# Weighted expert rows added to their tokens' rows by indirect DMAs, in place of stored rows and gathers

## What is computed

```python
x = x + cross_attention(layernorm(x), ctx)            # 16 heads, q and k with rms norm
h = layernorm(x)
# mixture of experts: E = 64 experts, K = 8 for each token, inner width 192
scores = softmax(h @ gate_weight.T)
topk_w, topk_idx = top_k(scores, 8);  topk_w = topk_w / sum(topk_w)
x = x + sum over k of topk_w[k] * (silu(h @ w_gate[e_k]) * (h @ w_up[e_k])) @ w_down[e_k]
# second layer
x = x + attention of layernorm(x) to the 256 context rows of its batch, masked
x = x + ternary feed-forward of layernorm(x), inner width 1408
```

## Time and profile before

| | |
|---|---|
| median of the runs | 1608.38 us (1607.07 to 1610.81, 3 runs) |
| the profiled execution | 1613.86 us |
| its span, first to last instruction | 1612.1 us |
| mean granted PE clock in the span | 0.936 of full |
| PE busy | 1428.4 us, 89% of the span |
| DVE, ACT, POOL busy | 1032.6, 905.1, 615.0 us (64%, 56%, 38%) |
| DMA queue of SP's loads and stores | 197.31 MB, 34.6% of 16 engines' span |
| DMA queue of POOL's indirect DMAs | 77.61 MB, 15.9% |

### The profile page before, as it was taken

The page is one execution under the profiler, slowest core; times in us unless marked ns, Lnnn a source line. Parts: engine busy times, 40 slices in busy tenths (PEclk is TensorE's granted clock), DMA queues, the critical chain, the costliest instruction groups (busy, mean ns, idle before and its releaser), DMA issues. The chain is left out here.

```text
span 1612.1 us, 37709 instructions
## 1 busy us (share of the span) xinstructions
PE 1428.4 (89%) x8673; PEld 1200.5 (74%) x8674; DVE 1032.6 (64%) x2067; ACT 905.1 (56%) x2048; POOL 615.0 (38%) x704
## 2 busy tenths in 40 slices
PE   7998899999843999999999999999943599999999
PEld 5887566667622898888888898888841488888888
DVE  5555488876696576777676765666635466676633
ACT  4554598873384566666666666666621244444442
POOL 1222287761142322322232232232226566666321
PEclk9999699999855999999999999999975799999999
DMA  6221592001171587778777877877537444444200
GB/s 209 85 85 53 213 359 90 2 5 53 53 307 57 180 261 270 269 252 283 261 278 255 284 236 252 269 255 240 194 129 249 131 144 141 124 125 130 78 13 28
DMA packets 93281, 278.16 MB, mean 173 GB/s; under 512 B 12757, under 2 KB 12886, under 8 KB 92502
## 3 DMA queue, kind: packets, MB, share of 16 engines
q1 hardware_dynamic: 68950, 197.31, 34.6%
q0 software_dynamic: 23680, 77.61, 15.9%
q10 hardware_dynamic: 576, 2.36, 0.4%
HBM read 209.07 MB, written 76.81 MB: 177 GB/s over the span
## 5 line engine op out<-in xcount | busy, mean ns | idle before, releaser
L1183 POOL DMA_INDIRECT xg<-h_rows,idx x168 | 183.9, 1095 | 467.5 <-PE m_x L1211 458.2
L1226 PE MATMUL m_g<-wgu_high,bxTh 128*128 x660 | 236.5, 358 | 3.7 <-DVE bxTl L1299 3.7
L1226 PE MATMUL m_g<-wgu_low,bxTh 128*128 x660 | 223.9, 339 | 0.0
L1226 PE MATMUL m_g<-wgu_high,bxTl 128*128 x660 | 223.8, 339 | 0.0
L1629 PE MATMUL f_g<-x4T_high,ffn_gu 128*128 128x256 f32 x704 | 177.0, 293 | 14.2 <-issue 12.2
L1299 DVE TENSOR_TENSOR bxTl<-m_x,bxTh 128x512 fp32r<-128x512 f32 x166 | 114.7, 691 | 88.4 <-ACT bxTh L1368 63.9
L1629 PE MATMUL f_g<-x4T_low,ffn_gu 128*128 128x256 f32 x704 | 169.9, 282 | 0.0
L1386 ACT ACTIVATE y<-m_y 128x512 f32<-128x512 f32 x164 | 98.1, 598 | 113.5 <-PE m_y L1246 87.3
L1061 DVE TENSOR_TENSOR wgu_low<-raw_gu,wgu_high x61 | 107.3, 1758 | 82.6 <-ACT wgu_high L1051 69.7
L1520 POOL DMA_INDIRECT G<-y_rows,slot x128 | 132.8, 1038 | 56.5 <-issue 50.5
L1246 PE MATMUL m_y<-wd_high,hidTm 128*128 x328 | 144.9, 442 | 7.6 <-issue 5.6
(11 more groups left out here) (264 smaller groups left out, 3310.6 us busy)
## 6 DMA issues: line engine op xcount, KB each, us to landing
raw_gu<-in_exp_gu SPq DMA_DIRECT2D x64, 768.0 KB, 6.6
y_rows<-y SPq DMA_DIRECT2D x164, 256.0 KB
raw_d<-in_exp_d SPq DMA_DIRECT2D x64, 512.0 KB, 7.4
y_rows<-zero SPq DMA_DIRECT2D x64, 256.0 KB, 3.4
ffn_gu<-ffn_gu_words SPq DMA_DIRECT2D x1, 5632.0 KB
raw_c<-in_ctxT SPq DMA_DIRECT2D x16, 256.0 KB, 2.7
X<-in_x SPq DMA_DIRECT2D x4, 1024.0 KB, 5.5
h_rows<-h SPq DMA_DIRECT2D x16, 256.0 KB, 2.0
```

The source lines that it names most:

```text
L1183: eng.indirect_dma_start(xg[:, u, :].bitcast(F32), None, h_dram, bass.IndirectOffsetOnAxis(ap=idx[half][:, u:u + 1], axis=0)).then_inc(s_g ...
L1226: m = eng.matmul(pg[u % 2][:, 0:2 * I], xT[l][:, u % 2, c, :], W.gu[r][:, buf * DC + c, :], start=c == 0 and n == 0, stop=c == DC - 1 and ...
```

## The change

In place of rows of experts stored once and gathered eight times a token, each expert's row is multiplied by its token's weight as ACT moves it out of PSUM, and added in DRAM to the row of its token.

- There are two sums in DRAM, `sums[0]` and `sums[1]`, of 2048 rows and 128 more. `attend` zeroes sum 1 and the extra rows; `route` stores X into sum 0 (16 more stores of 256 KB).
- `h_dram` has rows of 576 values: behind the 512 of h stand the token's 64 weights, one for each expert. `place` divides the exponentials L by their total (a product on POOL, where the marks were) and stores them there. DVE's search for the weights is gone; the total and its reciprocal come ahead of the lists. Padding rows now name one of the 128 extra rows, each its own (two more short operations for `blk_tok`).
- `experts`: a gather brings 576 values. POOL copies the column of the block's expert to `weight`; ACT scales by it. `y` has four slots and a fifth, in the space of X. In step b POOL issues the scatter-add of block b - 4, the weight copy of b and the gather of b + 4, in this order. Blocks with even u go to sum 0, with odd u to sum 1; a scatter waits until the last one to the same sum has landed. SP's stores are gone. POOL has four index tiles in place of two, and its loop holds four groups.
- `finish`: SP loads both sums of each tile by plain DMAs (32 of 256 KB): batch 0's first, 1's behind the small loads, those of 2 to 7 behind `load(1)`. DVE adds the two, one operation of 128x512 for each tile (16 in place of 128), and `find_exact` stands behind batch 0's norm. POOL has no DMAs there.

The core of the diff:

```diff
@@ attend, sync
-            for n in range(NBLK - T * K // P):
-                eng.dma_start(rest[n], zero[:, :]).then_inc(s_rest, 16)
+            for n in range(NT + 1):
+                eng.dma_start(sums[1][bass.ts(n, P), :], zero[:, :]).then_inc(s_rest, 16)
...
@@ route, sync
+                dveX.wait(eng, t, "x")
+                eng.dma_start(sums[0][bass.ts(t, P), :], X[:, t, :]).then_inc(s_sum, 16)
                 actH.wait(eng, t, "h")
-                eng.dma_start(h_dram[bass.ts(t, P), :], h[:, t % HBUF, :]).then_inc(s_h[t % HBUF], 16)
+                eng.dma_start(h_dram[bass.ts(t, P), 0:D], h[:, t % HBUF, :]).then_inc(s_h[t % HBUF], 16)
@@ place, gpsimd
-            eng.tensor_tensor(marked[:, :, :], mask16[:, :, :], order[:, :].unsqueeze(1).to_broadcast([P, NT, E]), ALU.mult).then_inc(s_mark, 1)
+            eng.tensor_tensor(L[:, :, :], L[:, :, :], winv[:, :].unsqueeze(2).to_broadcast([P, NT, E]), ALU.mult).then_inc(s_weight, 1)
@@ place, sync
+            eng.wait_ge(s_weight, 1)
+            eng.dma_start(h_dram.rearrange("(n p) d -> p n d", p=P)[:, 0:NT, D:D + E], L[:, :, :]).then_inc(s_weight, 16)
@@ place, vector
-            link(eng.tensor_copy(slot8[:, :, :], slot_f[:, :, :]))
+            eng.wait_ge(s_exp, 1)
+            link(eng.reduce_sum(total[:, :], e8[:, :, :], axis=AX.X))
+            link(eng.reciprocal(winv[:, :], total[:, :]))
...
-            words = L[:, :, :].bitcast(I32)
-            for n in range(2):
...
-                for t in range(NT):
-                    last = eng.max(found[n][:, t, :], both[:, t, :])
...
-            link(eng.tensor_tensor(blk_tok[:, :], plist[:, 1:NTAB + 1], below, ALU.subtract))
+            link(eng.tensor_tensor(listed[:, :], plist[:, 1:NTAB + 1], below, ALU.subtract))
+            link(eng.tensor_scalar(empty[:, :], listed[:, :], 0.0, part_f[:, 0:1], ALU.is_equal, ALU.mult))
+            link(eng.scalar_tensor_tensor(blk_tok[:, :], listed[:, :], float(T), empty[:, :], ALU.add, ALU.add))
@@ experts, sync
-                eng.dma_start(y_dram[bass.ts(b, P), :], y[:, u % 2, :]).then_inc(s_y[u % 2], 16)
@@ experts, gpsimd
+                poolW.wait(eng, (i - 1) * GB + u, "weight")
...
+            def weighted(i, u):
+
+                b = i * GB + u
+                e = eng.value_load(blk_tab[0:1, bass.ds((b + 2) * 2, 1)], min_val=0, max_val=E - 1)
+                eng.wait_ge(s_g[u], (i + 1) * 16)
+                actY.wait(eng, b - GB, "y")
+                apart(eng, s_apart)
+                poolW.done(eng.tensor_copy(weight[:, u:u + 1], xg[:, u, bass.ds(e + D, 1)].bitcast(F32)), "weight")
+
+            def scatter(i, u, at, last=False):
+
+                actY.wait(eng, i * GB + u, "y")
+                if not (isinstance(i, int) and i == 0 and u < 2):
+                    eng.wait_ge(s_y[u % 2], i * 32 + u // 2 * 16)
+                apart(eng, s_apart)
+                eng.indirect_dma_start(sums[u % 2], bass.IndirectOffsetOnAxis(ap=idx[at][:, u:u + 1], axis=0), y[:, GB if last and u == GB - 1 else u, :], None,
+                                       compute_op=ALU.add).then_inc(s_y[u % 2], 16)
+
+            def group(i, at, first):
+                for u in range(GB):
+                    if not first:
+                        scatter(i - 1, u, (at - 1) % IDX)
+                    weighted(i, u)
+                    gather(i + 1, u, (at + 1) % IDX)
+                name(i + 2, (at + 2) % IDX)
...
+            def later(i, at, last):
+                if not last:
                     with eng.If(i < groups):
+                        group(i, at, False)
+
+                with eng.If(groups > i - 1):
+                    with eng.If(groups < i + 1):
                         for u in range(GB):
+                            scatter(i - 1, u, (at - 1) % IDX, True)
@@ experts, scalar
                 peY.wait(eng, b, "y")
-                if stored is not None:
-                    eng.wait_ge(s_y[u % 2], stored)
-                actY.done(eng.activation(y[:, u % 2, :], py[u % 2][:, :], ACT.Copy), "y")
+                poolW.wait(eng, b, "weight")
+                if added is not None:
+                    eng.wait_ge(s_y[u % 2], added)
+                actY.done(eng.activation(y[:, u if at is None else at, :], py[u % 2][:, :], ACT.Copy, scale=weight[:, u:u + 1]), "y")
@@ finish, sync
+            def tokens(b):
+
+                for i in TI:
+                    t = b * TPB + i
+                    if b > 0:
+                        eng.wait_ge(s_g[i], 32 * b)
+                    eng.dma_start(X[:, t, :], sums[0][bass.ts(t, P), :]).then_inc(s_g[i], 16)
+                    eng.dma_start(G[:, t, :], sums[1][bass.ts(t, P), :]).then_inc(s_g[i], 16)
+
+            tokens(0)
             eng.dma_start(open8[:, :, :], a["mask"].unsqueeze(0).to_broadcast([P, B, S])).then_inc(s_m, 16)
...
+            tokens(1)
             eng.dma_start(Wdn[:, :, :].rearrange("p f d -> p (f d)").bitcast(F32), ffn_d).then_inc(s_ffn, 16)
             peC.wait(eng, 0, f"r{TPB - 1}")
             load(1)
+            for b in range(2, B):
+                tokens(b)
@@ finish, gpsimd
-            gather(0, places)
             Chain(nc, ctx, "f_poolc", eng)(eng.memset(minus_half[:, :], -0.5))
-            gather(1, places[:4])
             deviations_a(0)
-            gather(1, places[4:])
             deviations_4(0)
             deviations_a(1)
-            gather(2, places)
@@ finish, vector
-                dveA.done(eng.scalar_tensor_tensor(X[:, t, :], G[:, i, k, :], w8[:, t, k:k + 1], X[:, t, :], ALU.mult, ALU.add), f"k{k}_{i}")
+                    dveA.done(eng.tensor_tensor(X[:, t, :], X[:, t, :], G[:, t, :], ALU.add), f"sum{i}")
...
-            find_exact()
-            add(0, adds)
+            add(0)
             moments_a(0)
             scales_a(0)
             negatives(0)
-            add(1, adds[:6])
+            find_exact()
+            add(1)
             maxima(0)
```

More of the change, by code:

```diff
@@ L1166, in _ @@
                             one(i * GB + u, u)
-            for u in range(2):
-                eng.wait_ge(s_y[u], groups * 32 + 16)
-            apart(eng, s_apart)
         @block.gpsimd
@@ L1804, in one @@
                         beside[f](b + 1)
-                    if more2:
-                        add(b + 2, adds[n:n + ADDS.get(f, 0)])
-                        n += ADDS.get(f, 0)
+                    if more2 and f == 2:
+                        add(b + 2)
                 if more2:
```

170 lines of the change are left out of this document (67 added, 103 removed).

## The result

The changed kernel takes 1658.26 us (median of 4 runs, 1658.01 to 1662.04), against 1607.72 for the kernel before on the same chip: a ratio of 1.0318, 95% interval 1.0296 to 1.0341. It is slower; 1580.6 was forecast. The profiled execution has a span of 1656.0 us (before 1612.1), its mean granted PE clock is 0.934. The medians are 50.5 us apart and the spans 43.9, because the profiled execution of the kernel before was 6.1 us above that median. Cut at the same instructions in both traces, the difference of 43.9 us splits into

The account below looks back on a forecast made before the run. TensorE (PE) was taken to bound the experts' stage at 4.035 us a block, but not the stages around it. Terms -6.5 + 6 + 3.5 - 14.9 - 13.9 - 2.0 = -27.8 took 1608.38 to 1580.6 us, range 1562 to 1660.

Parts of the forecast that it names:

- 1, place: Between routing and experts: DVE's extraction of weights by bits goes, so the experts start earlier, -6.5 us.
- 2, experts: Experts' stage: POOL, DMA engines and scatter chain all stay below 4.035 us a block; +6 us charged for bursts.
- The chain's term: Experts' stage: a block costs at least half a scatter's issue-to-landing time L, taken as 5.5 us, half 2.75.
- The DMA term: Experts' stage: DMA engines' work per block for weights, gather and scatter, 3.22 to 4.12 us, taken as 3.6.
- rival B: Experts' stage: DMA engines fill, a second pass for adding makes a block 4.29 us, +41, 1616 us; chance 0.10.
- C, POOL is full: Experts' stage: an adding scatter costing over 2.6 us fills POOL, 4.75 us a block, +115, 1690 us; chance 0.07.
- A: Experts' stage: the scatter chain binds from L = 8.5 us; at 9.1 a block takes 4.55, 1658 us; chance 0.16.
- 3, the stage's end: End of the experts' stage: the last scatter lands later than a store did, +3.5 us (0.4 to 9).
- 4, start of the last stage: Last stage before its first feed-forward product: adds no longer wait for gathers, -14.9 us (-12 to -18).
- 5, batch 0: Last stage, batch 0: without gathers on POOL the 10.13 us idleness goes, -13.9 us (-8 to -15).
- 6, other batches: Last stage, later batches: PE already covers the adds, so removing gathers and adds gains little, -2.0 us (0 to -6).
- D: Batch 0: something other than POOL's queue holds the product back, so 13.9 us stay, 1594 us; chance 0.07.

Follow-up runs that it names:

- e1: Changed kernel with the weight copy and its register load moved from POOL to DVE, two blocks earlier in its order: 1625.0 us.
- e16: Changed kernel with POOL's order altered: weight copy before the scatter, then the gather: 1630.9 us, ratio 1.0171 to the kernel before.
- e3: Changed kernel with four sums in place of two, half of the experts' rows left out of the output: 1637.1 us.
- e6: Changed kernel with the weight copy on DVE and four sums, half of the experts' rows left out: 1595.6 us.
- e5: Changed kernel with DVE and ACT splitting only one of four gate and up chunks and one of two down chunks, output wrong: 1626.9 us.
- e10: Changed kernel with short splits on DVE and ACT and four sums, output neither the experts' nor whole: 1581.6 us.
- e11: Changed kernel with all scatters adding into one sum, each waiting for the one before: 1991.3 us.
- e9: Against the changed kernel: plain scatters to row 8 x token + rank in one chain, last stage loads eight rows a token and adds on DVE: 1796.1 us.
- e14: Rows-by-token version (plain scatters, adds in last stage) with two scatters in flight instead of one, and last-stage loads and find_exact reordered: 1637.1 us.
- e15: Rows-by-token version with two plain scatters in flight, POOL's loop unrolled for two groups in place of four: 1600.4 us.

## Why the prediction was wrong

**1, place: right** (-6.0 for -6.5).

**2, experts: the step that failed.** POOL's term was put at 2.85 to 3.8 us a block, both below 4.035, and so at nothing. It is 4.48 before any wait. One thing was mis-sized and one was left out. The adding scatter lay within its bounds (none to 0.95 more than a plain one; it is 0.6). "Copy and names some 0.35" is 0.75: without the copy the floor is 3.18 (e1), with it and the names 3.93. The register load costs nothing that shows; what costs is that the gather behind waits for POOL's own copy, 0.79 in place of 0.30 (e16 against the changed kernel), beside the copy's own 0.20. Put at 0.75, it would have moved the upper end to 4.2, above the block, and the step could not have been called safe. Left out were the stretches, 0.55 a block. The row was there: the earlier trace rows give a shortest gather of 944 ns, a median of 947 and a longest of 2503, and their mean is 1095 (1109 between 540 and 1150). As long as POOL had 2.8 us of slack in a block this cost nothing, and I read the usual length and not the tail. A step of 3.93 with 0.55 of disturbance can't keep a pace of 4.04.

**The chain's term** was L = 5.5, within 3.81 to 7.62; measured 6.78 (median 6.2), so the range held. What failed was to compare half of it with the mean of a block: the spread, up to 9.1 outside the loop's heads, lets it bind in bursts, for 20 us alone (e3) and for 27.6 once POOL is quick (e1 against e6).

**The DMA term** was 3.22 to 4.12, taken 3.6; by share times block it is 4.19 here, above that range, 4.04 to 4.18 in e1, e3, e5, e6 and e10 with the same traffic, and 3.13 without adding. So adding costs 0.9 to 1.06 us, at least as much as the whole plain scatter was put at (0.90). The rule quoted from the Trainium skill, Collectives: The Full Stack, section "The bandwidth ceiling: the fold count and why AG ≠ RS ≠ AR", about half the rate for an add in flight, gave a sum of 4.06; the trace agrees with it better than with my 3.6. Yet the engines ran at 0.97 and 0.98, so rival B, right that the engines would fill, was worth at most 6 us and not 41, and only after the others were gone.

**The point of decision** was 4.24 us a block. With the -41.8 measured outside it is 4.29 by (41.8 / 162), and 4.66 is beyond it by far. Of the rivals **C, POOL is full**, is what happened: 4.66 against its 4.75, 1658 against its 1690. It got 0.07 since its condition was put as an adding scatter of over 2.6 us. That was worked out from the losing point, 4.24 us. With the copy and the stretches counted, the condition is 4.24 - 0.55 - 0.75 - 1.30 - 0.30 = 1.3 us (1.30 is gather and its gap), and a plain scatter already takes 1.0. The number came close partly by luck: C had a scatter of 3.15 us with its gap, where 1.88 was measured, and no stretches and no wait for the copy. **A** named the number, 1658, by luck: its reason is worth 20 of 86 us (e3).

**3, the stage's end: right** (+3.0 for +3.5). **4, start of the last stage:** to PE's first turn, 30.4 to 17.0 us, the 13.4 forecast, by errors that cancel: the mask came 3.2 us later than before instead of 1.8, behind four loads, and the rest was shorter. The forecast itself had a slip: its terms add up to 1215.4, not 1215.9, so they give 13.9. From there on -6.3 in place of -1.5: a gap of 3.69 us on ACT ahead of the turned probabilities is 0.53 now, the products that read the context take 5.40 for 6.61, and the maxima wait for no adds. The trace doesn't say what that gap was. **5, batch 0: right**, 33.46 us from its first product to the first down product where 48.56 were, -15.1 for -13.9, and no gap of 10 us. (The 0.41 us of its first products stands in the trace but not in the earlier trace rows, which show 0.58 and 0.28.) **6, other batches:** -3.9 for -2.0, inside 0 to -6; three looped batches take 127.92, 42.64 each (1452.11 to 1580.03), so the adds were indeed covered. **D** didn't occur.

## What to carry to other kernels

An engine that gets new work has slack only after its worst instructions are counted: take the group's longest and its mean beside its usual length, and set the sum of the undisturbed step and of the disturbances against the pace it must keep. Limits that lie close together hide each other, so lift them in pairs before calling one of them small. Put another instruction between a small copy and the indirect DMA that must wait for it; that was worth 27 us here (e16).

## What the runs showed of the chip that was not expected

- An indirect DMA that adds occupies POOL for 1.58 us where a plain one takes 0.98 to 1.00, and a one-column copy behind it shows 0.77 instead of 0.19 us, 0.57 of it beside the scatter.
- Adding 256 KB in rows of 2 KB costs the 16 DMA engines 0.9 to 1.06 us more than writing them. In one chain, from one adding scatter to the next it is never under 5.35 us, 6.2 in the median (e11); plain ones had mostly landed within a block (e9: 43 waits in 113).
- POOL's indirect DMAs and copies are stretched by up to 1.6 us beside DVE's long two-input subtractions (1.22 and 1.76 us), and a stretched gather ends 0.9 us after the subtraction; with these cut short (and ACT's splits too), the mean stretch fell from 0.55 to 0.10 us a block at a higher DMA share.
- A loop body of four groups on POOL, a little longer than the changed kernel's, cost 2.4 to 6.6 us at each turn and doubled the packets of the instruction queue (e14); two groups did not (e15).
- The DMA engines hold a share of 0.97 to 0.98 over 610 us with 3.4 us of PE's waits for gathers at the most (e6, e10).
